# Attention maxima turned on VectorE instead of TensorE, row placing moved to GpSimd

## The chip, the cores and the metric

The kernel runs on one core of one Trainium2 chip. The metric is the device time of one launch in microseconds (us). The kernel before has a median of 676.17 us over 3 runs (671.06 to 678.32). Lower is better.

## The reference

Inputs are 8 sequences ("batches") of 512 tokens with 128 features. What is computed, all in float32:

```python
x = layernorm(x + attn(x))      # 16 heads of 8 features, softmax over 512 keys
# experts: 1 shared, 8 routed, 2 chosen for each token
gates = sigmoid(x @ Wg)
vals, idx = top_k(gates, 2);  vals = vals / vals.sum()
shared = silu(x @ Ws1) * (x @ Ws3) @ Ws2
routed = sum over chosen e of w[e] * (silu(x @ We1[e]) * (x @ We3[e])) @ We2[e]
out = layernorm(x + (shared + routed) / 3)
```

The 16 heads are made from the rows of the projection by a reshape, so a "head" of a batch is 32 tokens' worth of projected rows. The kernel works on them in groups of four: 32 groups in all, four for each batch.

## The kernel before, in words

The program is written engine by engine, with semaphores by hand. Its first part is attention, and a second part after it is the experts. `run_stages` gives every engine the same order: one *stage* (b, i) for each group, i = 0 to 3 within batch b, unrolled at both ends and a loop over batches 2 to 6 between. A stage has eight steps (`at` = 0 to 7).

In stage q = 4b + i TensorE does three things for three different groups. It computes the scores of group q+2 with queries on the partitions (`scoreA`, L1014), only so that VectorE can take their maxima per query (`mx`, L948). It computes the scores of group q with keys on the partitions (`scoreB`, L1028), for which two extra rows of the query stack `qs` hold the negated maximum in a high and a low bf16 part; ScalarE takes the exponential (L921). And in every odd step it multiplies group q-1's exponentials with the values (`pvp`, L1053). Beside these run *jobs* that share one PSUM bank `shared` in a fixed order (class `Jobs`): a job may overwrite the bank only when the job before it has been read. The job `mT` in step 1 turns the 128 x 16 maxima of group q+1 by a TensorE transpose (L532), and VectorE writes their high and low parts from PSUM to `m2` (L607, L609). Other jobs are `xT`, `qkv`, `valsT`, `oT`, `proj`, `x1T` (step 5 of i = 3, needs `x1`), `counts` (step 4 of i = 1) and `gate`.

The path of a group to its scores: the `qkv` job in step 6 of stage q makes queries and keys of group q+4; GpSimd splits them into three bf16 parts (L848 to L854) and adds the bias to the values (L863). In the next stage SyncE (SP) stores the parts to DRAM (L756), loads the maxima into `qs` (`load_maxima`, two transfers, L762), waits until the store has landed, and loads the stacks `qs` and `ks` (eight transfers, L778 and L782). `scoreA` of the stage after that waits for all eight. SP works strictly in this order; in stages i = 0 it also loads `xres` (four transfers) and stores `x1` (four transfers) behind the stacks, and these run into stage i = 1.

GpSimd's order within stage i: for i = 2 first `deviation` (L647, L649); for i = 3 a wait for that stage's stack loads and two indirect scatters of rows (L499, wait and all); then the split, the value bias; for i = 0 `copy_rows` and the `xres` bias; for i = 2 and 3 three more scatters each. The scatters write a batch's rows into expert slots. VectorE computes the slots: `choose` picks two experts for each token (eight pieces, two after every odd step of i = 0), `read_counts` copies the counts in step 4 of i = 1, and `place` turns them into slot numbers and carries the state on (five pieces in i = 1 and 2, L421 to L480). VectorE also normalizes `x1` in i = 3 (L639).

Of the kernel before, what the change touches and what calls it, by code (L numbers as in the profile page):

```python
# [50 lines left out]
class Jobs:  # L51
# [9 lines left out]
    def __init__(self, batches):  # L61
        self.quads = 4 * batches
        self.batches = batches
        self.index = {}
        n = 0
        for s in range(-4, self.quads + 4):
            for at in range(8):
                for kind, b, i in self.at(s // 4, s % 4, at):
                    self.index[kind, 4 * b + i] = n
                    n += 1  # L70
        self.total = n
        self.period = self.index["mT", 12] - self.index["mT", 8]

    def at(self, b, i, at):

        inner = not isinstance(b, int)
        s = 4 * b + i if not inner else 8
        early = not inner and s in (-2, -1)
        kinds = []
        if at == 0 and i == 2 and (inner or 1 <= b <= self.batches):  # L80
            kinds.append("proj")
        if at == 5 and i == 3 and (inner or 1 <= b <= self.batches):
            kinds.append("x1T")
        if at == 1 and (inner or 0 <= s + 1 < self.quads):
# [27 lines left out]
def layer(nc, x, w_qkv, b_qkv, w_out, b_out, wg, ws1, ws3, ws2, we1, we3, we2, out):  # L112
# [27 lines left out]
    with ctx:  # L140
# [47 lines left out]
        mx = sb("mx", [P, 2, 4, NCH])  # L188
        m2 = sb("m2", [16, 2, P], BF16)
        v_raw = sb("v_raw", [P, 4, NCH, HD])  # L190
# [76 lines left out]
        msplit_step = sem("msplit_step")  # L267
        m_loaded = sem("m_loaded")
        v_ready = sem("v_ready")
        b_ready = sem("b_ready")  # L270
# [13 lines left out]
        const_done = sem("const_done")  # L284
        route_step = sem("route_step")
        ids_done = sem("ids_done")
        scattered = sem("scattered")
# [4 lines left out]

        SPLITS = [(QUADS - 2, at) for at in (1, 3, 5, 7)] + [(QUADS - 1, at) for at in (1, 3, 5, 6, 7)]
        ROUTE_STEPS = 44
        CHOSEN = 14
        PLACED = 38

        def need(eng, s, value):
# [21 lines left out]
        def run_stages(eng, stage):  # L320
# [6 lines left out]
            for s in range(QUADS - 4, QUADS + 1):  # L327
                stage(s // 4, s % 4)

        def choose(dve, b, at):  # L330

            def done(n):
                dve.wait_ge(route_step, ROUTE_STEPS * b + n)

# [4 lines left out]
            if at == 0:  # L339

                dve.tensor_scalar(tmp[:], ge[:], 1.0, None, ALU.add).then_inc(route_step, 1)
                done(1)
# [46 lines left out]
        def read_counts(dve, b, bank, read):  # L389

            dve.wait_ge(route_step, ROUTE_STEPS * b + 17)
            dve.tensor_copy(before[:], bank[:, 0:NCH * E].rearrange("p (t e) -> p t e", e=E)) \
               .then_inc(route_step, 1)
            dve.wait_ge(route_step, ROUTE_STEPS * b + 18)
            dve.tensor_copy(count[:], bank[:, NCH * E:2 * NCH * E].rearrange("p (t e) -> p e t", e=E)) \
# [9 lines left out]
        def place(dve, b, at):  # L405
# [5 lines left out]
            def done(n):  # L411
                dve.wait_ge(route_step, ROUTE_STEPS * b + n)

# [56 lines left out]
            else:  # L470
# [10 lines left out]
                done(ROUTE_STEPS)  # L481

        def copy_rows(pool, b):

# [9 lines left out]
        def scatter_rows(pool, b, copies):  # L494

            need(pool, route_step, ROUTE_STEPS * b + PLACED)
            for n in copies:
# [10 lines left out]
        def pe_job(pe, kind, b, i):  # L508
# [6 lines left out]
            elif kind == "qkv":  # L515
# [6 lines left out]
                if has(b, i, 1):  # L522
                    for h in range(4):
                        for low in range(4):
# [3 lines left out]
                                            start=True, stop=True)  # L528
            elif kind == "mT":

                pe.wait_ge(max_done, 8 * (q + 2))
                ins = pe.transpose(shared[0:16, 0:P], mx[:, (i + 1) % 2].rearrange("p h q -> p (h q)"), ident[:])  # L532
            elif kind == "valsT":
# [16 lines left out]
            elif kind == "counts":  # L550
                pe.wait_ge(route_step, ROUTE_STEPS * (b - 2) + CHOSEN)
                ins = count_rows(pe, shared)
# [6 lines left out]
        def act_job(act, kind, b, i):  # L559
# [21 lines left out]
            elif kind == "gate":  # L581

                need(act, route_step, ROUTE_STEPS * (b - 2) + 1)
                act.activation(ge[:].rearrange("p t e -> p (t e)"), shared[:, 0:NCH * E], ACT.Exp,
                               scale=-1.0).then_inc(job_read, 1)

        def dve_job(dve, kind, b, i):
            q = 4 * b + i
            dve.wait_ge(job_ready, jobs.number(kind, b, i) + 1)
            if kind == "valsT":  # L590
# [6 lines left out]
                if i == 2:  # L597
# [5 lines left out]
                    .then_inc(job_read, 1)  # L603
            elif kind == "mT":

                need(dve, m_loaded, 32 * (q + 1))
                dve.tensor_scalar(m2[:, 0, :], shared[0:16, 0:P], -1.0, None, ALU.mult).then_inc(msplit_step, 1)  # L607
                need(dve, msplit_step, q + 2)
                dve.scalar_tensor_tensor(m2[:, 1, :], shared[0:16, 0:P], -1.0, m2[:, 0, :], ALU.mult,  # L609
                                         ALU.subtract).then_inc(job_read, 1)  # L610
            elif kind == "proj":
# [94 lines left out]
        def attention_sync(sp):  # L706
# [36 lines left out]
            def stage(b, i):  # L743
# [61 lines left out]
        def attention_gpsimd(pool):  # L805
# [27 lines left out]
            def stage(b, i):  # L833
                q = 4 * b + i
                if finishing(b) and i == 2:
                    deviation(pool, b)
                if scattering(b) and i == 3:
# [20 lines left out]
                if has(b, i, 1):  # L858
# [5 lines left out]
                                       bv[:, None].broadcast_to([P, 4, NCH, HD]), ALU.add).then_inc(v_ready, 1)  # L864

                if routing(b) and i == 0:
# [34 lines left out]
        def attention_scalar(act):  # L901
# [3 lines left out]
            def stage(b, i):  # L905
# [8 lines left out]
                for j in range(4):  # L914
                    for u in range(2):
# [7 lines left out]
                        for kind, bb, ii in jobs.at(b, i, 2 * j + u):  # L923
                            if kind not in ("valsT", "proj", "mT", "counts"):
                                act_job(act, kind, bb, ii)
# [8 lines left out]
        def attention_vector(dve):  # L934
# [8 lines left out]
            def stage(b, i):  # L943
                q = 4 * b + i
                for at in range(8):
                    if has(b, i, 2):
                        dve.wait_ge(a_ready, 8 * (q + 2) + at + 1)
                        dve.tensor_reduce(mx[:, i % 2, at // 2, at % 2 * 2:at % 2 * 2 + 2], scoreA[:, at % 2], AX.X,  # L948
                                          ALU.max).then_inc(max_done, 1)
                    for kind, bb, ii in jobs.at(b, i, at):  # L950
                        if kind in ("valsT", "proj", "mT"):
                            dve_job(dve, kind, bb, ii)
# [4 lines left out]
                    if i == 0 and at % 2 and routing(b):  # L957
                        if at == 1:
                            dve.wait_ge(job_read, jobs.number("gate", b - 1, 3) + 1)
                            dve.wait_ge(const_done, CONSTS)  # L960
                        choose(dve, b - 2, at - 1)
                        choose(dve, b - 2, at)
                    if i == 1 and at == 4 and routing(b):
                        read_counts_job(dve, b)
                    if i == 1 and at >= 5 and routing(b):
                        place(dve, b - 2, at - 5)
                    if i == 2 and finishing(b):
                        statistics(dve, b, at)
                    if i == 2 and at >= 5 and at % 2 and routing(b):
                        place(dve, b - 2, at // 2 + 1)  # L970
                    if i == 3 and finishing(b):
                        normalize(dve, b, at)
                    if isinstance(b, int) and (q, at) in SPLITS:
# [14 lines left out]
        def attention_tensor(pe):  # L988
# [11 lines left out]
            def stage(b, i):  # L1000
# [18 lines left out]
                def score_b(at, c):  # L1019

                    if has(b, i, 0):
                        j, kc = at // 2, at % 2 * 2 + c
                        if at == 0 and c == 0:

                            pe.wait_ge(m_loaded, 32 * (q + 1))

# [504 lines left out]
        def moe_tensor(pe):  # L1531
# [14 lines left out]
            def beside(n):  # L1546
# [3 lines left out]
                if n == COUNT_AT:  # L1550

                    pe.wait_ge(job_read, jobs.total)
                    pe.wait_ge(route_step, ROUTE_STEPS * (B - 1) + CHOSEN)
                    count_rows(pe, shared).then_inc(counts_ready, 1)
# [147 lines left out]
```

## Time and profile before

| what | value |
|---|---|
| median of 3 runs | 676.17 us (671.06 to 678.32) |
| the profiled execution, its own time | 675.15 us |
| its span, first to last instruction | 673.4 us |
| mean granted TensorE clock | 0.978 |
| PE busy | 631.1 us, 94% |
| VectorE busy | 547.1 us, 81% |
| ScalarE busy | 426.1 us, 63% |
| GpSimd busy | 269.0 us, 40% |

The span is one execution on the chip. "Busy" is the time in which at least one instruction of that engine was under way; matmuls overlap, so a busy PE is not a PE at its peak. PE is the matmul, PEld its weight load, DVE VectorE, ACT ScalarE, POOL GpSimd, SPq the transfers that SyncE issues. Idle time of an engine stands in brackets with what ended it. Attention runs from the start to about 489 us, the experts from there to the end.

### The profile page before, as it was taken

To read this page: it belongs to the slowest core of one execution; us is meant where nothing else is said; L and a number is where in the kernel's file an instruction comes from. 1 tells how busy PE (TensorE), PEld (TensorE's weight loads), DVE (VectorE), ACT (ScalarE), POOL (GpSimd) and SP (SyncE) were. 2 spreads that over 40 slices of the span, in tenths; PEclk is the share of its full clock that TensorE was granted. 3 is DMA by queue.
4 is the path that set the end of the run, shared out by engine and by line. 5 is a ranking of instruction groups with operands and counts; after the bars stand their busy time and mean duration, and the time that the engine had idled before them with its cause. 6 is when DMAs were issued, how large, how long until landed. Compare 5 with 4: busy or idle time off the path is not lost.

```text
span 673.4 us, 16169 instructions
## 1 busy us (share of the span) xinstructions
PE 631.1 (94%) x4643; PEld 321.9 (48%) x4643; DVE 547.1 (81%) x1271; ACT 426.1 (63%) x970; POOL 269.0 (40%) x403
## 2 busy tenths in 40 slices
PE   7899899999999999999999999999899989999990
PEld 4443333433433433343343334423248878888880
DVE  4897677879897997999899799888648757788884
ACT  2066577777676776767776776776744336676672
POOL 3313112232144335414443531450524416677774
PEclk7999899999999999999999999999979999999996
DMA  4557646444433423533333343240231032446433
GB/s 84 124 118 168 139 115 141 105 84 106 74 77 89 93 51 71 104 78 77 75 78 58 84 99 77 63 95 2 59 115 52 29 80 84 119 119 181 133 110 106
DMA packets 161969, 62.61 MB, mean 93 GB/s; under 512 B 110570, under 2 KB 155628, under 8 KB 161920
## 3 DMA queue, kind: packets, MB, share of 16 engines
q1 hardware_dynamic: 155008, 46.66, 32.4%
q0 software_dynamic: 5616, 13.26, 6.6%
q10 hardware_dynamic: 1296, 2.10, 0.9%
q8 instruction: 24, 0.39, 0.3%
q14 instruction: 25, 0.20, 0.1%
HBM read 37.97 MB, written 24.19 MB: 92 GB/s over the span
## 4 chain that ended last, share of the span: by engine, by line
PE 61%; DVE 9%; DMA 9%; issue 8%; POOL 6%; SPq 4%; ACT 3%; POOLq 0%; ACTq 0%; DVEq 0%
PE pvp L1053 16%; PE scoreB L1028 14%; PE scoreA L1014 13%; DVE mx L948 4%; DMA parts_dram<-parts 4%; POOL y_dram L1246 4%; ACT prob L921 2%; PE shared L536 2%; DMA prob<-y_dram 2%; PE scoreB L1643 2%; PE shared L525 1%; PE pvp L997 1%; DMA ks<-parts_dram 1%; PE shared L544 1%; SPq L782 1%
## 5 line engine op out<-in xcount | busy, mean ns | idle before, releaser
L948 DVE TENSOR_REDUCE mx<-scoreA 128x2 f32<-128x1024 f32 x256 | 306.6, 1219 | 60.6 <-PE scoreA L1014 57.6
L921 ACT ACTIVATE prob<-scoreB 128x512 f32<-128x512 f32 x512 | 278.4, 599 | 118.5 <-PE scoreB L1028 118.1
L1014 PE MATMUL scoreA<-ks,qs 72*128 72x512 bf16 x512 | 193.9, 384 | 7.5 <-DMA ks<-parts_dram 4.9
L1028 PE MATMUL scoreB<-qs,ks 74*128 74x512 bf16 x512 | 195.0, 383 | 4.7 <-ACT prob L921 2.1
L1053 PE MATMUL pvp<-prob,v 128*32 128x512 f32 x1024 | 139.2, 617 | 0.8 <-ACT pv_sb L913 0.8
L1014 PEld LDWEIGHTS scoreA<-ks,qs 72*128 72x128 bf16 x512 | 49.4, 99 | 141.0 <-DVE mx L948 55.9
L1028 PEld LDWEIGHTS scoreB<-qs,ks 74*128 74x128 bf16 x512 | 49.3, 98 | 79.5 <-ACT prob L921 54.0
L1246 POOL DMA_INDIRECT y_dram<-prob x71 | 69.8, 983 | 42.0 <-issue 27.3
L499 POOL DMA_INDIRECT slots_dram<-rows,slot_i x64 | 63.2, 988 | 56.4 <-DMA ks<-parts_dram 31.3
L848 POOL CAST parts<-qk 128x256 bf16<-128x256 f32 x32 | 12.7, 397 | 176.2 <-ACT v_raw L574 165.0
L1643 PE MATMUL scoreB<-w,prob 128*128 x284 | 43.4, 276 | 0.3 <-DVE prob L1432 0.3
L1503 ACT ACTIVATE prob<-scoreA 128x256 f32<-128x256 f32 x71 | 27.3, 384 | 24.7 <-PE pvp L1631 12.3
L1053 PEld LDWEIGHTS pvp<-prob,v 128*32 128x32 f32 x1024 | 20.4, 108 | 36.3 <-issue 34.7
L1643 PEld LDWEIGHTS scoreB<-w,prob 128*128 128x128 f32 x284 | 37.2, 191 | 0.5 <-issue 0.5
L1621 PE MATMUL scoreA<-w_high,ebT_high 128*128 x71 | 34.0, 479 | 1.5 <-DVE gated L1436 1.5
L1510 ACT ACTIVATE prob<-scoreB,prob 128x128 f32<-128x128 f32 x71 | 26.1, 368 | 11.4 <-PE scoreA L1601 10.3
L570 ACT ACTIVATE qk<-shared,bq 128x128 f32<-128x128 f32 x64 | 20.0, 364 | 18.3 <-PE shared L525 10.7
L1436 DVE TENSOR_TENSOR gated<-scoreA,prob 128x256 f32<-128x256 f32 x71 | 29.7, 419 | 1.4 <-ACT prob L1503 1.3
L647 POOL TENSOR_SCALAR veps<-mv 128x4 f32<-128x4 f32 x8 | 1.8, 228 | 70.1 <-DVE mv L629 70.1
L1358 DVE TENSOR_TENSOR ebT_low<-scoreA,ebT_high 128x128 fp32r<-128x128 f32 x71 | 20.5, 290 | 11.3 <-ACT ebT_high L1477 9.2
L1623 PE MATMUL scoreA<-w_high,ebT_low 128*128 x71 | 28.0, 394 | 0.0
L1622 PE MATMUL scoreA<-w_low,ebT_high 128*128 x71 | 27.9, 393 | 0.0
(178 smaller groups left out, 918.2 us busy)
## 6 DMA issues: line engine op xcount, KB each, us to landing
qs<-parts_dram SPq DMA_DIRECT2D x96, 96.0 KB
parts_dram<-parts SPq DMA_DIRECT2D x32, 192.0 KB
slots_dram<-blank POOLq DMA_DIRECT2D x9, 520.0 KB
prob<-slots_dram SPq DMA_DIRECT2D x71, 65.0 KB, 1.9
ks<-parts_dram SPq DMA_DIRECT2D x64, 64.0 KB
prob<-y_dram SPq DMA_DIRECT2D x7, 512.0 KB
ks<-parts_dram SPq DMA_DIRECT2D x32, 96.0 KB
xin<-in_L_attn_x SPq DMA_DIRECT2D x32, 64.0 KB, 2.3
```

The lines of the kernel that those rows point to most:

```text
L499: pool.indirect_dma_start(slots_dram, bass.IndirectOffsetOnAxis(ap=slot_i[:, j, t:t + 1], axis=0), rows[:, t, j, :], None).then_inc(scatte ...
L921: act.activation(prob[:, i % 2, j, 2 * u + c, :], scoreB[:, c], ACT.Exp, scale=SCALE).then_inc(exp_done, 1)
L948: dve.tensor_reduce(mx[:, i % 2, at // 2, at % 2 * 2:at % 2 * 2 + 2], scoreA[:, at % 2], AX.X, ALU.max).then_inc(max_done, 1)
L1014: ins = pe.matmul(scoreA[:, at % 2, c], qs[0:KR, st, j, qc * P:(qc + 1) * P], ks[0:KR, st, j, :], start=True, stop=True)
L1028: pe.matmul(scoreB[:, c], ks[0:KM, i, j, kc * P:(kc + 1) * P], qs[0:KM, i, j, :], start=True, stop=True).then_inc(b_ready, 1)
L1053: ins = pe.matmul(pvp[32 * h:32 * h + 32, :], v[:, (i - 1) % 2, h, j, :], prob[:, (i - 1) % 2, h, j, :], start=(j == 0), stop=(j == 3))
L1246: pool.indirect_dma_start(y2_dram, bass.IndirectOffsetOnAxis(ap=eb[:, at, D:D + 1].bitcast(I32), axis=0), yo[:, r, :], None, bounds_check= ...
L1436: dve.tensor_tensor(gated[:, r % 4, :], h_bank(r)[:, F:2 * F], silu[:, r % 2, :], ALU.mult) \
L1621: pe.matmul(h, ebT_highs[:, r % 4], high, start=True, stop=False)
L1622: pe.matmul(h, ebT_highs[:, r % 4], low, start=False, stop=False)
L1623: ins = pe.matmul(h, ebT_lows[:, r % 4], high, start=False, stop=True)
L1643: ins = pe.matmul(y_bank(r), gatedT[:, (r - 4) % 4, c * P:(c + 1) * P], w2_flat[:, bass.ds(e * NFC * D + c * D, D)], start=(c == 0), stop= ...
```

## The change

- The job `mT` goes. `turn_maxima` takes its place at step 0 of the stage: VectorE writes the high and low parts of the 128 x 16 maxima from SBUF to `m2` (now 128 x 32) and turns `m2` in blocks of 32 x 32 into `mT`. `load_maxima` reads `mT` in four transfers of 32 rows of 64 bytes each, not two of 16 rows of 256 bytes.
- `choose` is spread over i = 0 and i = 1.
- For all batches but the last two, `place` goes from VectorE to GpSimd: `place_rows` in stage i = 1 (33 instructions, 27 waits on its own steps), `move_state` behind the scatters of i = 3 (8 instructions). The last two batches keep the VectorE version.
- For batches that end inside the attention part, `x1` is normalized on GpSimd in i = 2, and `deviation` moves there too, both behind the split and the value bias.

```diff
-            kinds.append("mT")
...
+        def turn_maxima(dve, q, parity):
+            maxima = mx[:, parity].rearrange("p h q -> p (h q)")
+            dve.wait_ge(max_done, 8 * (q + 1))
+            need(dve, maxima_turned, q)
+            dve.tensor_scalar(m2[:, 0, :], maxima, -1.0, None, ALU.mult).then_inc(msplit_step, 1)
+            need(dve, msplit_step, 2 * q + 1)
+            dve.scalar_tensor_tensor(m2[:, 1, :], maxima, -1.0, m2[:, 0, :], ALU.mult, ALU.subtract) \
+               .then_inc(msplit_step, 1)
+            need(dve, msplit_step, 2 * q + 2)
+            need(dve, m_loaded, 64 * q)
+            dve.transpose(mT[:], m2[:].rearrange("p m x -> p (m x)")).then_inc(maxima_turned, 1)
...
-                    sp.wait_ge(job_read, jobs.number("mT", b, i) + 1)
-                    for m in range(2):
-                        sp.dma_start(qs[KR + m:KR + m + 1, (i + 1) % 4].rearrange("p h x -> p (h x)"), m2[:, m, :]) \
-                          .then_inc(m_loaded, 16)
+                    sp.wait_ge(maxima_turned, 4 * b + i + 2)
+                    rows = qs[KR:KR + 2, (i + 1) % 4].rearrange("m h (c j t) -> m (h c) j t", c=NCH, j=4)
+                    for low in range(4):
+                        sp.dma_start(rows[:, :, low], mT[32 * low:32 * low + 32, :]).then_inc(m_loaded, 16)
...
-                if finishing(b) and i == 2:
-                    deviation(pool, b)
...
+                if finishing(b) and i == 2:
+                    deviation(pool, b)
+                    need(pool, rstd_done, b)
...
+                    for c in range(NCH):
+                        ins = pool.tensor_scalar(x1[:, c, :], res[:, c, :], mv[:, c, 0:1], rstd[:, c:c + 1],
+                                                 ALU.subtract, ALU.mult)
+                    ins.then_inc(x1_done, 1)
                 if routing(b) and i == 0:
                     copy_rows(pool, b - 2)
+                if scattering(b) and i == 1:
+                    need(pool, const_done, CONSTS)
+                    place_rows(pool, b - 2)
                 if scattering(b) and i >= 2:
                     scatter_rows(pool, b - 2, SCATTERED_AT[i, 1])
+                if scattering(b) and i == 3:
+                    move_state(pool, b - 2)
...
+        CHOSEN_AT = {(0, 1): (0, 1), (0, 3): (2, 3), (0, 5): (4,), (0, 7): (5,), (1, 1): (6,), (1, 3): (7,)}
```

The new `place_rows`, cut: every `op` is one GpSimd `tensor_tensor`, and `done(n)` a wait for its n-th step.

```python
pool.memset(scan, 0.0); pool.memset(cum[:, :, 0:1], 0.0)
pool.tensor_copy(cum[:, :, 1], count[:, :, 0])
done(3); op(cum[:, :, 2], cum[:, :, 1], count[:, :, 1], ALU.add)
done(4); op(cum[:, :, 3], cum[:, :, 2], count[:, :, 2], ALU.add)
done(5); op(held2[:], held[:], cum[:, :, 3], ALU.add)
done(6); op(held2[:], held2[:], count[:, :, 3], ALU.add)
...
done(31); op(slot[:], sel[:, :, :, 0], sel[:, :, :, 1], ALU.add)
done(32); pool.tensor_copy(slot_i[:], slot[:]).then_inc(slots_placed, 1)
```

## Rows read from the trace of the kernel before

**Rows 1.** Windows, i = 0 to 3: length, busy PE PEld DVE ACT POOL, clock, DMA.

```profile
380.89:394.35 13.46, 13.35 (x108) 4.84 (x107) 12.44 (x25) 9.93 (x22) 5.62 (x9) 1.00 0.42 93
394.35:409.25 14.90, 14.60 (x116) 5.75 (x115) 13.70 (x32) 10.51 (x23) 5.85 (x12) 1.00 0.40 84
409.25:423.36 14.11, 14.11 (x115) 5.89 (x114) 13.38 (x30) 9.91 (x22) 3.31 (x7) 1.00 0.33 61
423.36:438.35 14.99, 14.87 (x119) 6.15 (x118) 12.09 (x21) 10.68 (x24) 7.38 (x10) 1.00 0.33 71
```

**Rows 2.** Waits over the span: us in total, times, longest.

```profile
PEld scoreA L1014 <- DVE mx L948: 55.9, 72, 1.5
POOL slots_dram L499 <- DMA ks<-parts_dram: 31.3, 5, 6.5
PE scoreA L1014 <- DMA ks<-parts_dram: 4.9, 5, 2.2
```

**Rows 3.** Timeline, PE around a turned maximum and around none: start, length.

```profile
382.52 0.39 PE L1028 MATMUL scoreB<-qs,ks 74*128 74x512 bf16 x1
...
382.95 1.06 PE L1053 MATMUL pvp<-prob,v 128*32 128x512 f32 x8
383.94 0.10 PEld L1014 LDWEIGHTS scoreA<-ks,qs 72*128 72x128 bf16 x1 [0.84 <-DVE mx L948]
...
394.12 0.10 PEld L1014 LDWEIGHTS scoreA<-ks,qs 72*128 72x128 bf16 x1 [0.84 <-issue]
...
399.52 0.38 PE L1028 MATMUL scoreB<-qs,ks 74*128 74x512 bf16 x1
399.83 0.64 PE L1053 MATMUL pvp<-prob,v 128*32 128x512 f32 x4
```

**Rows 4.** Groups by line in that batch: busy us, mean ns.

```profile
L609 DVE SCALAR_TENSOR_TENSOR m<-shared,m 16x128 bf16<-16x128 f32 x4 | 1.1, 278 | 0.1
```

**Rows 5.** Timeline of SyncE's transfers, stages i = 0 and 1.

```profile
383.25 0.38 SPq L756 DMA_DIRECT2D parts_dram<-parts  x1
384.43 1.93 SPq L762 DMA_DIRECT2D qs<-m  x2
387.23 1.18 SPq L778 DMA_DIRECT2D qs<-parts_dram  x3
...
398.01 0.39 SPq L756 DMA_DIRECT2D parts_dram<-parts  x1
398.51 2.60 SPq L762 DMA_DIRECT2D qs<-m  x2
401.99 1.16 SPq L778 DMA_DIRECT2D qs<-parts_dram  x3
```

**Rows 6.** Timeline, a stage whose end waits for its stack loads.

```profile
173.34 1.16 SPq L778 DMA_DIRECT2D qs<-parts_dram  x3
...
179.13 0.39 PE L1014 MATMUL scoreA<-ks,qs 72*128 72x512 bf16 x1 [0.58 <-DMA ks<-parts_dram]
```

**Rows 7.** Groups by line, small GpSimd instructions: busy us, mean ns.

```profile
L863 POOL TENSOR_TENSOR v<-v_raw,bv 128x128 f32<-128x128 f32 x32 | 14.7, 458 | 21.8 <-ACT valsT L578 11.1 <-issue 10.7
L1233 POOL TENSOR_TENSOR prob<-prob 128x4 f32<-128x4 f32 x7 | 1.5, 210 | 0.6
```

**Rows 8.** Timeline of GpSimd around stages i = 1 to 3.

```profile
410.44 0.46 POOL L863 TENSOR_TENSOR v<-v_raw,bv 128x128 f32<-128x128 f32 x1
420.36 1.05 POOL L649 TENSOR_TENSOR rstd<-veps,half 128x4 f32<-128x4 f32 x1 [0.18 <-POOL veps L647]
422.61 0.40 POOL L848 CAST parts<-qk 128x256 bf16<-128x256 f32 x1 [1.20 <-ACT v_raw L574]
435.59 0.96 POOL L499 DMA_INDIRECT slots_dram<-rows,slot_i  x1 [6.04 <-DMA ks<-parts_dram]
```

**Rows 9.** Timeline of VectorE beside a GpSimd instruction with two inputs.

```profile
406.90 0.21 DVE L444 TENSOR_TENSOR pos<-before,cum 128x32 f32<-128x32 f32 x1
408.44 0.67 DVE L450 TENSOR_TENSOR tmp<-pos,room 128x32 f32<-128x32 f32 x1
```

More of the change, by code:

```diff
@@ L268, in layer @@
         m_loaded = sem("m_loaded")
+        maxima_turned = sem("maxima_turned")
         v_ready = sem("v_ready")
@@ L481, in place, with place_rows, done, per_expert @@
                 done(ROUTE_STEPS)
+        def place_rows(pool, b):
+            def done(n):
+                need(pool, place_step, PLACE_STEPS * b + n)
+            def per_expert(ap):
+                return ap[:, :, None].broadcast_to([P, E, NCH])
+            def by_tile(ap):
+                return ap[:, None, :].broadcast_to([P, NCH, E])
+            def op(out, x, y, what):
+                pool.tensor_tensor(out, x, y, what).then_inc(place_step, 1)
+            scan = g2[:].rearrange("p t e -> p (t e)")[:, 0:2 * (4 + E)].rearrange("p (a x) -> p a x", a=2)
+            first = sel[:, 0].rearrange("p t e -> p (t e)").rearrange("p (e t) -> p e t", t=NCH)
+            need(pool, job_read, jobs.number("counts", b + 2, 1) + 1)
+            pool.memset(scan, 0.0).then_inc(place_step, 1)
+            pool.memset(cum[:, :, 0:1], 0.0).then_inc(place_step, 1)
+            pool.tensor_copy(cum[:, :, 1], count[:, :, 0]).then_inc(place_step, 1)
+            done(3)
+            op(cum[:, :, 2], cum[:, :, 1], count[:, :, 1], ALU.add)
+            done(4)
+            op(cum[:, :, 3], cum[:, :, 2], count[:, :, 2], ALU.add)
+            done(5)
+            op(held2[:], held[:], cum[:, :, 3], ALU.add)
+            done(6)
+            op(held2[:], held2[:], count[:, :, 3], ALU.add)
+            op(first, cum[:], per_expert(held[:]), ALU.add)
+            done(7)
+            op(shift2[:], held2[:], room[:], ALU.subtract)
+            done(9)
+            op(fits[:], per_expert(shift2[:]), limits[:, None, :].broadcast_to([P, E, NCH]), ALU.subtract)
+            op(pos[:], before[:], first.rearrange("p e t -> p t e"), ALU.add)
+            done(10)
+            pool.tensor_scalar(fits[:], fits[:], 0.0, None, ALU.is_gt).then_inc(place_step, 1)
+            done(11)
+            op(tmp[:], pos[:], by_tile(room[:]), ALU.subtract)
+            done(12)
+            op(fits[:, :, 0:2], fits[:, :, 0:2], fits[:, :, 2:4], ALU.add)
+            done(13)
+            pool.tensor_scalar(tmp[:], tmp[:], 0.0, None, ALU.is_ge).then_inc(place_step, 1)
+            done(14)
+            op(more[:], fits[:, :, 0], fits[:, :, 1], ALU.add)
+            op(scan[:, 0, 4:], fits[:, :, 0], fits[:, :, 1], ALU.add)
+            done(15)
+            op(pos[:], pos[:], by_tile(shift[:]), ALU.add)
+            done(17)
+            op(scan[:, 1, 4:], scan[:, 0, 4:], scan[:, 0, 3:3 + E], ALU.add)
+            done(19)
+            op(scan[:, 0, 4:], scan[:, 1, 4:], scan[:, 1, 2:2 + E], ALU.add)
+            done(20)
+            op(ends[:], scan[:, 0, 4:], scan[:, 0, 0:E], ALU.add)
+            done(21)
+            op(ends[:], ends[:], end[:].broadcast_to([P, E]), ALU.add)
+            done(22)
+            op(shift2[:], ends[:], more[:], ALU.subtract)
+            done(23)
+            pool.tensor_scalar(shift2[:], shift2[:], float(P), None, ALU.mult).then_inc(place_step, 1)
+            done(24)
+            op(shift2[:], shift2[:], room[:], ALU.subtract)
+            done(25)
+            op(shift2[:], shift2[:], shift[:], ALU.subtract)
+            done(26)
+            op(tmp[:], tmp[:], by_tile(shift2[:]), ALU.mult)
+            done(27)
+            op(pos[:], pos[:], tmp[:], ALU.add)
+            done(28)
+            op(sel[:], hot[:], pos[:, None].broadcast_to([P, TOP_K, NCH, E]), ALU.mult)
+            done(29)
+            op(sel[:, :, :, 0:4], sel[:, :, :, 0:4], sel[:, :, :, 4:8], ALU.add)
+            done(30)
+            op(sel[:, :, :, 0:2], sel[:, :, :, 0:2], sel[:, :, :, 2:4], ALU.add)
+            done(31)
+            op(slot[:], sel[:, :, :, 0], sel[:, :, :, 1], ALU.add)
+            done(32)
+            pool.tensor_copy(slot_i[:], slot[:]).then_inc(slots_placed, 1)
@@ new lines, in move_state, with done @@
+        def move_state(pool, b):
+            def done(n):
+                need(pool, place_step, PLACE_STEPS * b + n)
+            used, added = fits[:, :, 0], fits[:, :, 2]
+            pool.tensor_scalar(used, more[:], 0.0, None, ALU.is_gt).then_inc(place_step, 1)
+            pool.tensor_scalar(added, more[:], float(P), None, ALU.mult).then_inc(place_step, 1)
+            done(33)
+            pool.tensor_tensor(shift2[:], shift2[:], used, ALU.mult).then_inc(place_step, 1)
+            done(34)
+            pool.tensor_tensor(room[:], room[:], added, ALU.add).then_inc(place_step, 1)
+            done(35)
+            pool.tensor_tensor(shift[:], shift[:], shift2[:], ALU.add).then_inc(place_step, 1)
+            pool.tensor_copy(held[:], held2[:]).then_inc(place_step, 1)
+            pool.tensor_copy(end[:], ends[:, E - 1:E]).then_inc(place_step, 1)
+            pool.tensor_copy(all_ends[:, bass.ds(b, 1), :], ends[:, None, :]).then_inc(place_step, 1)
+            done(PLACE_STEPS)
@@ L945, in stage @@
                 for at in range(8):
+                    if at == 0 and has(b, i, 1):
+                        turn_maxima(dve, q + 1, (i + 1) % 2)
                     if has(b, i, 2):
```

71 lines of the change are left out of this document (40 added, 31 removed).

## The prediction

> **What bounds the kernel now.** I read the busy times first (the table above), then the windows of one batch, then the waits, then the timeline of single stages. PE is busy 94% of the span, VectorE 81%. One batch of the loop takes 57.46 us in four stages, 13.46 + 14.90 + 14.11 + 14.99, and in each PE is busy for all but 0.0 to 0.3 us, while VectorE has 12.09 to 13.70 us to do [rows 1]. So PE is full and VectorE nearly. The waits seem to blame VectorE: `scoreA` waits 55.9 us, 72 times, for the maxima [rows 2]. But the single wait is always 0.84 us, with VectorE named or with nothing named [rows 3]: it is the time that the four `pvp` matmuls in front of it take (382.95 to 383.94), and a late maximum would lengthen it. In the loop VectorE holds nothing up; work taken from it is worth nothing there by itself.
>
> What stands close behind PE is the path of a group's stacks. Where it ends last it holds `scoreA` up, 4.9 us in 5 waits over the span [rows 2], and GpSimd waits for the same loads before its scatters in i = 3, 31.3 us in 5 waits. How near it is in the loop: SP stores the parts at 383.25 and issues the first stack load at 387.23, 3.98 us later [rows 5]. In a stage that did wait, the first load went out at 173.34 and `scoreA` started at 179.13, 5.79 us later [rows 6]. For i = 0 that gives 387.23 + 5.8 = 393.0, and `scoreA` started at 394.12 [rows 3]: 1.1 us to spare. For i = 1, 401.99 + 5.8 = 407.8 against 409.25 - 0.2: 1.3 us.
>
> **Part 1, the turned maxima.** On PE one transpose goes from each stage. From the last `scoreB` to `pvp` it was 0.43 us with it (382.52 to 382.95) and 0.31 without a job (399.52 to 399.83) [rows 3]: 0.12 us a stage, 32 x 0.12 = 3.8 us. In i = 1 the next job no longer waits for VectorE to read the bank; the stage's PE is idle for 14.90 - 14.60 = 0.30 us [rows 1], I allow half, 0.15, six times, 0.9 us. So PE gives back 4.7 us at most.
>
> On VectorE the two reads of PSUM (0.28 each [rows 4]) give way to three dependent small instructions in front of the first maximum. A small one takes 0.21 alone and 0.67 beside a GpSimd instruction with two inputs [rows 9], and GpSimd's split runs just then (422.61 on, against the stage at 423.36 [rows 8, 1]). So 0.6 to 2.0 us, against 0.56 before; VectorE's load falls anyhow (part 3), and I cost it at nothing. If its cover went, `scoreA` of step 2 would be late, by at most 1 us a stage. The Trainium skill ("SBUF — State Buffer", the two separate sides) says that this pair of ports is locked for a whole instruction, and against either engine; the 0.67 agrees for VectorE, and no row shows GpSimd held up.
>
> On SP two transfers become four, between the parts' store and the stack loads. The rows say what they cost: after the store at 398.01 the two ended at 401.11 (398.51 + 2.60), after that at 383.25 they ended at 386.36, both 3.1 us after the store, though issued 0.5 and 1.2 us after it [rows 5]. So SP is held to about 2.5 us behind the store and then takes 0.6 us each. Four end at 3.1 + 2 x 0.62 = 4.34 us, and with 0.2 us for the next wait the loads start 4.55 us behind the store, not 3.98: **0.57 us later in each stage**. Bounds: 0 (if the small transfers cost half as much) and 1.2 us (all of them behind the landing). I take 0.57, the nearest rows.
>
> **Part 2, the stage path with that.** Stages i = 2 and 3 have room and gain PE's 0.12 each. In i = 3 the stack lands 0.57 later and GpSimd's two scatters (435.59 on [rows 8]) with it, and the next stage starts 0.12 earlier: the split of i = 0, which starts when they are done, and the store move from 2.36 us into the stage (383.25 - 380.89) to 3.05. From store to the next stage is 4.55 + 5.8 = 10.35, so i = 0 takes 13.40, PE alone asks for 13.34. In i = 1 the store comes where SP gets to it, 14.76 us behind that of i = 0 (398.01 - 383.25), now 15.33. Both stages together: 3.05 + 15.33 + 10.35 = 28.73 us against 28.36 (13.46 + 14.90). Stages i = 2 and 3: 14.11 + 14.99 - 0.24 = 28.86. The batch: 57.59 against 57.46. **What PE gives, SP takes back: +0.1 us a batch**, for five batches 0.7 us. Ahead of the loop the five waits for stacks [rows 2] would each grow by 0 to 0.57; I take two of them, 1.1 us, less 7 stages at 0.12, 0.8. The last batch, almost without stacks to load, keeps PE's gain: 4 x 0.12 + 0.15 = -0.6. Parts 1 and 2: 0.7 + 1.1 - 0.8 - 0.6 = +0.4, between -4.7 (nothing of SP's shows) and +5 x 1.4 (all 1.2 us show).
>
> **Part 3, placing on GpSimd.** 33 instructions: 19 of 8 elements or about that at 0.21, 11 of 32 or 64 at 0.27 to 0.33 (between 0.210 for 4 and 0.458 for 128 elements [rows 7]), 3 others at 0.2: 7.6 us. Of the 27 waits 19 follow right on the awaited step, and such a gap is 0.18 (420.36 [rows 8]): 3.4 us. Sum 11.0; bounds 8.7 (all at 0.19, fewer gaps) and 14.3 (all at 0.27, 27 gaps of 0.2). It starts behind the value bias at 410.90 and must be over when the split of i = 2 begins, 422.61 [rows 8]: 11.7 us, 11.55 with a stage 0.15 shorter. So it just fits. Each us beyond delays that split, the stack, the scatters, the split of i = 0 and thus the two full stages: one us a batch, five times. I take it 0.3 us over, for its first wait (0.18) and operands in three dimensions, whose price no row shows: +1.4. By the rule on the ports it would be held up besides, by each two-input instruction of VectorE that it meets.
>
> The normalization (4 x 0.35 estimated from 0.458 for 128 elements with two inputs) and `deviation` (1.5) follow the bias and end some 5.6 us into i = 3; `x1T` stands at step 5, over 7 us in. Covered. `move_state` (8 x 0.21 + 4 x 0.18 = 2.4) ends 10 us into i = 0, before the split at 12.6. What VectorE loses (about 6 us of `place` and 1.3 of `x1` a batch) covered nothing. The experts' part keeps its VectorE version and does not move.
>
> **Sum.** 675.15 (the profiled execution, 1.0 below the median) + 0.4 + 1.4 = **677 us**, no change within 1%, which is about what a measurement of this kernel can tell.
>
> **Rivals.**
> 1. *GpSimd's placing does not fit* (slower). From 11.55 us on each us costs 5. At 14.3 it is 2.7 us over: 675.5 + 5 x 2.75 = 689. Its place is the split of i = 2 at 422.61. For it: the length is built of waits, and at about 13.5 us `x1T` loses its cover too. Against: the sum of 11.0. Chance 0.30.
> 2. *SP's extra transfers hide* (faster, a little). They are ready early and cost under 0.3 us each: then PE's 4.7 us stay, 675.15 - 4.7 = 670.5; a little less waiting ahead of the loop brings it to 668. For it: the landing of the store, not the issue, ends most waits. Against: the 0.6 us of rows 5. Chance 0.20.
> 3. *VectorE was the bound after all* (faster by over 1%). If the stages i = 1 and 2, where it is busy 13.70 of 14.90 and 13.38 of 14.11 [rows 1], shrank by 0.8 each: 675 - 6 x 1.6 - 4.7 = 661. Against it the constant 0.84. The Trainium skill ("GPSIMD Engine Reference", when to use it) puts elementwise work on VectorE as the faster one, which speaks against the move, not for it. Chance 0.08.
> 4. Forecast as worked out: 0.42.
>
> **How the numbers follow.** Within 1% (668.4 to 681.9) lie the forecast, most of rival 2 and the mildest of rival 1: 0.42 + 0.13 + 0.02 = 0.57. Faster: rival 3 and the best of rival 2, 0.08 + 0.07 = 0.15. Slower: the rest of rival 1, 0.28. The range 667 to 690 leaves out rival 3 and the worst of rival 1.
>
> **What would show it.** After: `mx` as late as before against `scoreA`; the first stack load 4.5 us behind the store; i = 0 and 1 together 28.4 to 29 us with `scoreA` waiting for the stacks; GpSimd's placing 10.5 to 12 us long, ending near the split. The forecast is wrong if the stack loads still start 4.0 us behind the store, if the placing is over 12.5 us, or if i = 1 gets under 14.5 us.

## The result: 0.6% slower, and the profile after

The changed kernel takes 679.62 us (median of 20 runs, 671.87 to 682.71), the kernel before, timed on the same chip, 675.33 us (20 runs, 670.98 to 682.92). The ratio is 1.0063 with a 95% interval of 1.0042 to 1.0085: slower by about 4 us, within the 1% that counts as no change. The forecast was 677 us and no change.

The profiled execution of the changed kernel took 682.71 us, its span is 681.0 us; it is the longest of the 20 runs, and about 3 us of its span come from a longer stretch at half clock near the start, told of below. So the loop's stages are compared, not the spans. First the windows of one batch after, columns as in [rows 1]:

```profile
387.04:401.22 14.18, 13.32 (x106) 4.74 (x105) 12.50 (x24) 10.51 (x22) 8.62 (x20) 1.00 0.39 82
401.22:416.25 15.03, 14.40 (x114) 5.75 (x114) 12.18 (x21) 10.45 (x22) 5.55 (x11) 1.00 0.41 90
416.25:430.16 13.91, 13.91 (x114) 5.81 (x114) 11.75 (x21) 9.66 (x22) 8.41 (x38) 1.00 0.31 62
430.16:445.04 14.88, 14.77 (x118) 6.13 (x117) 11.35 (x16) 10.68 (x24) 10.61 (x15) 1.00 0.35 67
```

Stages i = 2 and 3 are 0.20 and 0.11 us shorter than before, as PE's missing transposes would have it. Stages i = 0 and 1 are 0.72 and 0.13 longer, although PE works less in them (13.32 and 14.40 against 13.35 and 14.60 [rows 1]): 0.86 us of i = 0 is idle PE, 0.11 before. Over the four, VectorE is busy 3.8 us less (47.78 against 51.61) and GpSimd 11.0 us more (33.18 against 22.16).

The waits over the span (columns as in [rows 2]) name what PE is idle for:

```profile
PE scoreA L1147 <- DMA ks<-parts_dram: 12.9, 14, 2.3
PEld scoreA L1147 <- DVE mx L1084: 40.6, 48, 1.7
```

`scoreA` waits for the stack loads 14 times, 12.9 us, where it was 5 times and 4.9 us [rows 2]. The wait for the maxima, 55.9 us before, is smaller; as then, most of these are the constant 0.84 of `pvp`. In the timeline of PE, at the end of i = 0:

```profile
399.62 0.61 PE L1186 MATMUL pvp<-prob,v 128*32 128x512 f32 x4
400.98 0.39 PE L1147 MATMUL scoreA<-ks,qs 72*128 72x512 bf16 x1 [0.75 <-DMA ks<-parts_dram]
```

SyncE's transfers in the same two stages, to be read against [rows 5], and its stack loads in i = 3:

```profile
390.43 0.39 SPq L876 DMA_DIRECT2D parts_dram<-parts  x1
390.95 4.00 SPq L883 DMA_DIRECT2D qs<-mT  x4
395.30 1.17 SPq L898 DMA_DIRECT2D qs<-parts_dram  x3
...
406.00 0.40 SPq L876 DMA_DIRECT2D parts_dram<-parts  x1
406.51 3.62 SPq L883 DMA_DIRECT2D qs<-mT  x4
410.49 1.17 SPq L898 DMA_DIRECT2D qs<-parts_dram  x3
...
438.20 1.84 SPq L902 DMA_DIRECT2D ks<-parts_dram  x5
```

From the store to the first stack load it is 4.87 and 4.49 us, where it was 3.98 and 3.98 [rows 5]. The four transfers end 4.52 and 4.13 us behind the store, and 0.35 later the first load goes out. Last, GpSimd's new work, first and last lines of placing (33 instructions), then what follows:

```profile
417.48 0.12 POOL L518 MEMSET g<- 128x24 f32 x1
...
424.58 0.20 POOL L513 TENSOR_TENSOR shift<-shift 128x8 f32<-128x8 f32 x1 [0.18 <-POOL shift L513]
424.96 0.25 POOL L513 TENSOR_TENSOR tmp<-tmp,shift 128x32 f32<-128x32 f32 x1 [0.18 <-POOL shift L513]
...
427.51 0.19 POOL L577 CAST slot_i<-slot 128x8 int32<-128x8 f32 x1 [0.17 <-POOL slot L513]
429.41 0.40 POOL L966 CAST parts<-qk 128x256 bf16<-128x256 f32 x1 [1.71 <-ACT v_raw L688]
...
434.66 3.14 POOL L992 TENSOR_SCALAR x<-res,mv,rstd 128x128 f32<-128x128 f32 x4 [0.64 <-POOL rstd L769]
...
443.57 0.96 POOL L617 DMA_INDIRECT slots_dram<-rows,slot_i  x1 [1.92 <-DMA ks<-parts_dram]
...
445.78 0.41 POOL L966 CAST parts<-qk 128x256 bf16<-128x256 f32 x1
```

Placing takes 427.70 - 417.48 = 10.2 us and is over 1.71 us before the split of i = 2 can begin. The split of i = 0 starts at 445.78, 0.74 us into the stage; before, it started 0.53 us ahead of it. (On average over four batches: 0.56 into the stage, and 0.37 ahead of it before.)

### The profile page after: what moved, and what is told of

Read it like the earlier page. It is cut to its first block, busy times and chain, and to the rows that moved or that the text cites. A ratio compares the mean times of both kernels' runs of the same rounds, so it can differ in the third digit from the quotient of the medians.

```text
span 681.0 us, 16556 instructions
## 1 busy us (share of the span) xinstructions
PE 630.9 (93%) x4613; PEld 321.4 (47%) x4613; DVE 527.1 (77%) x1119; ACT 427.6 (63%) x970; POOL 344.1 (51%) x677
## 3 DMA queue, kind: packets, MB, share of 16 engines
q0 software_dynamic: 5616, 13.26, 6.8%
## 4 chain that ended last, share of the span: by engine, by line
PE 44%; SPq 16%; DMA 11%; issue 10%; POOL 8%; DVE 7%; ACT 3%; POOLq 0%; ACTq 0%; DVEq 0%
PE pvp L1186 10%; PE scoreB L1161 9%; PE scoreA L1147 9%; SPq L883 6%; DMA ks<-parts_dram 5%; POOL y_dram L1379 3%; DMA parts_dram<-parts 3%; SPq L902 3%; DVE mx L1084 3%; SPq L898 2%; DMA prob<-y_dram 2%; POOL slots_dram L617 2%; SPq L775 2%; ACT prob L1055 2%; SPq L912 2%
## 5 line engine op out<-in xcount | busy, mean ns | idle before, releaser
L1147 PE MATMUL scoreA<-ks,qs 72*128 72x512 bf16 x512 | 194.8, 386 | 15.6 <-DMA ks<-parts_dram 12.9
L1643 ACT ACTIVATE prob<-scoreB,prob 128x128 f32<-128x128 f32 x71 | 26.1, 368 | 11.4 <-PE scoreA L1734 10.2
L1047 ACT ACTIVATE pv_sb<-pvp 128x512 f32<-128x512 f32 x31 | 18.5, 597 | 12.9 <-PE pvp L1186 12.9
```

The costliest lines, as they stand in the source:

```text
L1147: ins = pe.matmul(scoreA[:, at % 2, c], qs[0:KR, st, j, qc * P:(qc + 1) * P], ks[0:KR, st, j, :], start=True, stop=True)
```

## The experiments

The theories. **S**: SP's four transfers, which stand between the parts' store and the stack loads, take PE's gain and more. **G**: GpSimd's placing and normalization take it. **V**: work taken from VectorE is worth something. Kernels that were timed side by side share the runs of the kernel before; each ratio is to those. "Batch" is the mean of the four loop batches from stage 12 to stage 27, four stages each: 57.48 us before, 58.33 after.

**1. The turned maxima alone**, everything else as before:

```diff
-                pe.wait_ge(max_done, 8 * (q + 2))
-                ins = pe.transpose(shared[0:16, 0:P], mx[...], ident[:])
+                        turn_maxima(dve, q + 1, (i + 1) % 2)
-                    for m in range(2):
-                        sp.dma_start(qs[KR + m:KR + m + 1, ...], m2[:, m, :])
+                    for low in range(4):
+                        sp.dma_start(rows[:, :, low], mT[32 * low:32 * low + 32, :])
```

> The kernel before with the turned maxima and SP's four transfers alone; choice, placing and x1 stay on VectorE as before. Theory S (SP's four transfers make the stacks late in i = 0 and 1): the cost is here. First stack load 4.5 to 4.9 us behind the store, i = 0 and 1 together 28.7 to 29.2 us (before 28.36), i = 2 and 3 0.1 shorter each; ratio to before 1.002 to 1.007. Theory G (GpSimd's longer list of work makes the split late): as before or faster by PE's 0.12 us a stage, ratio 0.994 to 0.999.

Measured: 676.77 us (12 runs) against 672.95, ratio 1.0068 (1.0032 to 1.0103). The whole loss is in this part. The four transfers, the loads and the waits are those of the whole change:

```profile
386.67 0.39 SPq L758 DMA_DIRECT2D parts_dram<-parts  x1
387.19 4.00 SPq L765 DMA_DIRECT2D qs<-mT  x4
391.54 1.17 SPq L780 DMA_DIRECT2D qs<-parts_dram  x3
```

```profile
PE scoreA L1018 <- DMA ks<-parts_dram: 12.2, 14, 1.7
```

Store to load is 4.87 us and the batch 58.30.

**2. The moves alone**: placing, `x1` and the state on GpSimd, the choice over two stages, and the maxima turned on TensorE as before.

```diff
+            kinds.append("mT")
...
-                        turn_maxima(dve, q + 1, (i + 1) % 2)
```

> The change without the turned maxima: the transpose stays on TensorE with two transfers, while the choice is spread, and the placing and x1 go to GpSimd. Theory S: nothing of it is on the path, ratio 0.998 to 1.002, stages as before to 0.1 us, first stack load 3.98 us behind the store. Theory G: the slowdown is here, ratio 1.004 to 1.008, with the split of i = 2 or of i = 0 later than before. Theory V (VectorE was a bound): faster, i = 1 and 2 shorter by 0.5 us or more, ratio under 0.99.

Measured: 672.98 us against 672.95, ratio 0.9987 (0.9962 to 1.0012). G falls, and V with it for the stages of the loop. The window of its stage i = 1, columns as in [rows 1]:

```profile
395.23:410.05 14.82, 14.44 (x115) 5.83 (x114) 11.69 (x20) 10.55 (x23) 5.83 (x12) 1.00 0.43 89
```

VectorE has 2.0 us less to do in i = 1 (11.69 against 13.70 [rows 1]) and the stage is 0.08 us shorter. One stage outside the loop does gain from the moves: stage 29, in the last batch, takes 13.26 us instead of 14.29.

**3. The whole change with the four transfers issued by ScalarE**, one in each of steps 1 to 4, behind the exponentials of the step:

```diff
-                if has(b, i, 1) and not ramp:
-                    load_maxima()
+                        if has(b, i, 1) and 2 * j + u in (1, 2, 3, 4):
+                            if 2 * j + u == 1:
+                                act.wait_ge(maxima_turned, q + 2)
+                            low = 2 * j + u - 1
+                            act.dma_start(rows[:, :, low], mT[32 * low:32 * low + 32, :])
```

> The changed kernel with its four transfers of the maxima issued by ScalarE's queue, one behind each of steps 1 to 4, not by SP. Theory S: the first stack load is again 4.0 us behind the store, the waits for stacks in i = 0 and 1 go, a batch takes 56.7 to 57.0 us, ratio to before 0.990 to 0.996. Theory G: as the changed kernel, 1.004 to 1.008. A cost of its own is possible: each issue holds ScalarE up by some tenths of a us, and scoreB waits for its exponentials.

Measured: 670.31 us against 672.95, ratio 0.9959 (0.9922 to 0.9996), with a batch of 56.84 us and the loads on average 4.0 to 4.2 us behind the store. With SP's four transfers gone the loss turns into a gain: S again.

**4. Two transfers ahead of the store, two behind**, both still on SP. Behind a store SP issues nothing for about 2.5 us anyway, so two transfers there should be free.

```diff
+                if has(b, i, 1) and not ramp:
+                    load_maxima(range(2))
                 if has(b, i, 3):
...
-                    load_maxima()
+                    load_maxima(range(2, 4))
```

> The changed kernel with two of SP's four transfers ahead of the parts' store and two behind it. Theory S: behind the store it is as before, first stack load 4.0 us after it; but the two ahead take 1.3 us of SP where SP is late already (i = 1), so the store of i = 1 comes as much later as its stack load comes earlier. i = 0 shorter by 0.5 to 0.9 against the changed kernel, i = 1 as there; ratio to before 0.998 to 1.004, below the changed kernel's 1.006. Theory G: 1.004 to 1.008.

Measured: 685.71 us (6 runs), ratio 1.0191 (1.0143 to 1.0239): a miss. The loads do start 3.97 us behind the store, but the store of i = 1 is late itself:

```profile
395.23 0.39 SPq L886 DMA_DIRECT2D parts_dram<-parts  x1
399.20 1.18 SPq L900 DMA_DIRECT2D qs<-parts_dram  x3
...
409.29 0.38 SPq L834 DMA_DIRECT2D xin<-in_L_attn_x  x1
409.77 1.41 SPq L875 DMA_DIRECT2D qs<-mT  x2
411.45 0.40 SPq L886 DMA_DIRECT2D parts_dram<-parts  x1
```

The two ahead (409.77 to 411.18) stand in front of a store whose parts GpSimd had finished at 407.06: the distance between the two stores is 16.22 us, 14.76 before and 15.57 after. i = 1 takes 16.14 us. That SP comes late to the store of i = 1 was in the expectation; it had i = 0 shorter and i = 1 as in the changed kernel. On average i = 0 takes 13.38 us (14.20 after) and i = 1 16.33 (15.36): together 29.71 against 29.56. The store of i = 1 comes a set distance behind that of i = 0 (16.22 to 16.28 us in four batches), whenever the stage begins, so what i = 0 gains i = 1 loses, and nothing is left. Stage i = 2 is 0.8 us longer on average: it takes 15.5 us in the two of four batches where a stretch of 3.4 us at half clock lies in it, 13.9 in the others. Two more such stretches lie ahead of stage 12 (65.5 and 123.5), where the kernel before, from stage 0 on, has one (80.4). In i = 1, issues ahead of the store cost in full; those behind it are free up to its landing: with two of them the loads start 3.98 us behind it, as in the kernel before.

**5. Each of the four transfers in two halves**, eight issues:

```diff
                     for low in range(4):
-                        sp.dma_start(rows[:, :, low], mT[32 * low:32 * low + 32, :])
+                        for m in range(2):
+                            part = mT[32 * low + 16 * m:32 * low + 16 * m + 16, :]
+                            sp.dma_start(rows[m:m + 1, :, low], part)
```

> The changed kernel with each of SP's four transfers of the maxima cut in two (16 rows of 64 bytes each): same bytes, eight issues. Theory S: SP pays about 0.65 us for each issue beyond the first, so the first stack load is 7.2 to 7.6 us behind the store (changed kernel 4.6 to 4.9); all of i = 0, 1 and 3 wait for stacks, a batch takes 63 to 68 us, 700 to 720 us in all. If bytes or rows were what costs, not issues: as the changed kernel, 679.

Measured: 744.91 us (2 runs), ratio 1.1059 (1.1008 to 1.1109).

```profile
436.08 0.38 SPq L876 DMA_DIRECT2D parts_dram<-parts  x1
436.57 6.40 SPq L885 DMA_DIRECT2D qs<-mT  x8
443.32 1.16 SPq L900 DMA_DIRECT2D qs<-parts_dram  x3
```

Store to load 7.24 us, 2.37 more than with four: 0.6 us for each issue more. The batch has 66.66 us. The step was as expected; the total lies higher. The granted clock of the run is 0.927, against 0.977 in the change: in time at half clock that is an estimated 54 us lost ((1 - 0.927) x 743) instead of 16, and the 38 us between them bring the 745 to 707 (more on the clock below).

**6. The turned maxima alone, from ScalarE's queue**: experiment 1 with the transfers of experiment 3, nothing moved to GpSimd.

> The kernel before with the turned maxima alone, their four transfers issued by ScalarE's queue. Theory S: what TensorE gives (0.12 us a stage and some tenths in i = 1) is kept, ratio 0.993 to 0.998, as the variant with the moves to GpSimd; the moves are worth nothing. Theory V (work taken from VectorE counts once SP is out of the way): slower than that variant by 0.3% or more.

Measured: 671.27 us against 673.90, ratio 0.9946 (0.9921 to 0.9971), not to be told from experiment 3. But its batch is 57.32 us and that of experiment 3 56.84, so the pair was timed again (9 and 10).

**7. The kernel before, with its two transfers issued by ScalarE** in steps 2 and 3, TensorE turning the maxima:

```diff
-                        sp.dma_start(qs[KR + m:KR + m + 1, (i + 1) % 4]..., m2[:, m, :])
+                            act.dma_start(qs[KR + m:KR + m + 1, (i + 1) % 4]..., m2[:, m, :])
```

> The kernel before, its TensorE transpose kept, with its two transfers of the maxima issued by ScalarE's queue. If SP's queue was on the path before the change too: ratio 0.994 to 0.998, and the turned maxima are worth little by themselves. Theory S as the prediction has it (1.1 us to spare in i = 0 and 1 before): 0.999 to 1.001 in the loop; only the stages that waited for stacks gain.

Measured: 676.18 us against 673.90, ratio 1.0005 (0.9966 to 1.0043). Loads on average 3.97 to 4.04 us behind the store, as before. So two transfers were hidden by the store, and another queue alone brings nothing; what experiments 3 and 6 gain is PE's.

**8. Placing made longer** by eight dependent additions on GpSimd (128 x 8 each, their result is not used):

```diff
+            for k in range(EXTRA):
+                op(cum[:, :, 3], count[:, :, 3], count[:, :, 3], ALU.add)
+                done(k + 1 - EXTRA)
             pool.memset(scan, 0.0).then_inc(place_step, 1)
```

> The changed kernel with eight more dependent GpSimd instructions at the head of the placing (8 x 0.39 = 3.1 us, their results are not used): 10.2 becomes 13.3 us, 1.6 to 1.8 us more than fits ahead of the split of i = 2. By the prediction's term of one us a batch for each us too much, five times: +8 to +9 us on the changed kernel, a batch 60 us, 687 in all. If the wait for the stack in i = 3 (1.9 us in the changed kernel) takes it up: under +2 us.

Measured: 688.06 us (4 runs), ratio 1.0245 (1.0195 to 1.0295), 1.8% over the change; batch 60.77 us.

```profile
433.16 0.19 POOL L581 CAST slot_i<-slot 128x8 int32<-128x8 f32 x1 [0.17 <-POOL slot L514]
433.61 0.40 POOL L970 CAST parts<-qk 128x256 bf16<-128x256 f32 x1 [0.26 <-issue]
...
438.88 3.16 POOL L996 TENSOR_SCALAR x<-res,mv,rstd 128x128 f32<-128x128 f32 x4 [0.64 <-POOL rstd L773]
```

```profile
442.18 0.63 PE L667 MATMUL shared<-ident,x 128*128 128x128 f32 x4 [1.46 <-POOL x L996]
```

```profile
PE shared L667 <- POOL x L996: 5.4, 6, 1.5
```

The split of i = 2 now starts right behind the placing, 1.28 us into i = 3 instead of 0.75 ahead of it. So everything behind it on GpSimd is 2.03 us later. The split itself hardly shows (i = 0 takes 14.40 us on average, 14.20 after); what shows is `x1T`, which lost its cover. After, it had 0.6 us to spare (`x1` ready at 437.80, turned from 438.39); 2.03 - 0.59 = 1.44, and the wait is 1.46. Stage i = 3 takes 15.94 us on average against 14.86. With i = 0 that is 1.3 us a batch. Of the rest of the batch's 2.4 us, 0.9 is one stage i = 1, with a stretch of 10.2 us at half clock from 400.1 on: it takes 19.33 us, the other three 15.57 on average, and the 3.8 between them are spread over four batches. The other 0.2 is in these three (15.57 against 15.36 after).

**9 to 11. Experiment 3, experiment 6 and the change itself, side by side**, to price the moves once SP is out of the way.

> The whole change with the four transfers of the turned maxima issued from ScalarE's queue (the kernel of the third experiment), now timed side by side with the same without the moves to GpSimd. Theory M (the moves are worth something once SP is out of the way): in the profile of the version without them, PE waits 0.49 us longer for a maximum in each stage i = 1, because VectorE's choice pieces at the end of i = 0 and its turn stand in front of the first maximum. With the moves there is no such wait: i = 1 takes 14.72 against 15.20, five loop batches and a few ends, 2.4 to 3 us. So this one at 0.992 to 0.996 of before and 0.3 to 0.5% faster than its partner. Rival N (GpSimd's placing and normalization give it back elsewhere): both alike within 0.1%.

> Turned maxima from ScalarE's queue, placing, normalization and choice as before (the kernel of the sixth experiment). Theory M: 0.3 to 0.5% slower than its partner, 0.996 to 0.999 of before, batch 57.3 us, with the wait of 0.49 us in each i = 1. Rival N: within 0.1% of its partner.

> The changed kernel itself beside these two: 1.005 to 1.008 of before again, and 1.0 to 1.4% over the version with ScalarE's transfers, if SP's four transfers are its whole loss. A profile without a long stretch at half clock near the start should show the span at 674 to 678.

Measured, 12 runs each against 672.98 us: with the moves 668.05, ratio 0.9938 (0.9913 to 0.9962); without them 672.03, 0.9989 (0.9958 to 1.0020); the change 678.13, 1.0067 (1.0038 to 1.0095). The moves are worth 0.5% here, V after all. Experiments 3 and 6, the same two kernels timed apart, did not show it (0.9959 and 0.9946, each known to some 0.3%), so the size rests on this pair and on the traces. The window of i = 1 with the moves, then without:

```profile
388.30:403.01 14.71, 14.32 (x114) 5.74 (x113) 12.65 (x23) 10.55 (x23) 5.93 (x12) 1.00 0.41 90
```

```profile
389.20:404.40 15.20, 14.40 (x114) 5.81 (x113) 14.12 (x33) 10.50 (x23) 5.87 (x12) 1.00 0.42 86
```

Only i = 1 differs, by 0.49 us; i = 0 takes 13.35 us in both. Its start without the moves, on VectorE and then on PE:

```profile
389.01 0.18 DVE L375 TENSOR_TENSOR hot<-iota_e,pick 128x32 f32<-128x32 f32 x1
...
390.40 0.17 DVE L612 TENSOR_SCALAR m<-mx 128x16 bf16<-128x16 f32 x1
390.61 0.57 DVE L614 SCALAR_TENSOR_TENSOR m<-mx,m 128x16 bf16<-128x16 f32 x1
391.31 0.21 DVE L618 STREAM_TRANSPOSE mT<-m 128x32 bf16<-128x32 bf16 x1
391.45 3.46 DVE L946 TENSOR_REDUCE mx<-scoreA 128x2 f32<-128x1024 f32 x3
```

```profile
392.71 0.39 PE L1012 MATMUL scoreA<-ks,qs 72*128 72x512 bf16 x1 [0.50 <-DVE mx L946]
```

The choice runs into i = 1, then comes the turn, and the first maximum starts 2.25 us into the stage; PE then waits 0.50 us for it. With the moves the choice is spread over two stages, the first maximum starts at 389.40, 1.10 us in, and PE does not wait. From stage 12 on this happens five times (4 x 0.49, and 0.49 in the last batch), 2.5 us, and stage 11 takes 15.80 instead of 14.85: 3.4 of the 4.0 us between the medians. Experiment 9 is also the version that beats both kernels: 0.6% under the one before, and 1.3% under the change by the two ratios (0.9938 / 1.0067).

## Why the forecast was right, step by step

The sum was near (677 against 679.6), and the mechanism that was named likeliest is the one that the runs show: SP takes back more than PE gives. That the sum came so near is in part luck: the batches were put 3.7 us too low and the placing 1.4 us too high.

- **PE is the bound, VectorE holds nothing up.** Right for the loop of the kernel before (experiment 2: no stage there shrinks by more than 0.1 us). It has its limit: with the turn on VectorE and no moves it holds i = 1 up by 0.49 us. The turn was costed at nothing because the moves free VectorE; the price without that cover is within the "at most 1 us a stage" of the forecast.
- **PE's gain**, 4 x 0.12 + 0.15 = 0.63 us a batch. Experiment 9 against before: 57.46 - 56.83 = 0.63 (0.11, 0.19, 0.19 and 0.14 by stage). On average 0.07 of it comes with the moves alone (experiment 2).
- **SP, 4.55 us from store to load instead of 3.98.** Measured 4.87 in i = 0 and 4.49 in i = 1 of the batch above (4.88 and 4.61 on average). The term was mis-sized twice: the four take up to 4.52 us, not 4.34, and the wait behind them 0.35, not 0.2. Rival 2 (they hide) is refuted.
- **The store of i = 0 at 3.05 us.** It came at 3.39, and over four batches at 3.58 (3.37 to 3.92). This is the step that was off most, and for the most part by its start: the 2.36 us of the batch in [rows 5] are the earliest of the four before, which are 2.93, 2.59, 2.89 and 2.36, on average 2.69. So the store moved by 0.89, where 0.69 was forecast. In i = 3 the last stack load is issued 9.88 us into the stage (438.20 + 1.84 - 430.16), before it was 9.16 in, 0.72 later and not 0.57. The scatters start 13.41 us in (443.57 - 430.16), before 12.23 (435.59 - 423.36 [rows 8, 1]); over four batches 13.20 and 12.39, 0.81 later. The loads of that stage before:

```profile
430.69 1.83 SPq L782 DMA_DIRECT2D ks<-parts_dram  x5
```

  From the last issue to the scatter it is 3.53 us here and 3.07 in the batch before, but over four batches it is 3.17 to 3.53 and 3.03 to 3.58, on average 3.33 and 3.23: the landing takes hardly longer, it only varies.
- **Store to next stage 5.8 us behind the load.** 401.22 - 395.30 = 5.92 and 416.25 - 410.49 = 5.76. Right.
- **i = 0 and 1 together 28.73 us, the batch 57.59.** 29.21 in the batch shown, 29.56 on average; the batch 58.33. The 0.83 by its parts: 0.53 from the store of i = 0, 0.24 from the distance between the stores (15.57, not 15.33), the rest from the last load. Five batches make 3.7 us more than forecast.
- **Ahead of the loop +0.3, last batch -0.6.** Up to stage 12 the change, run again, took 207.09 us and the kernel before 208.44; the profiled run of after took 211.72, with 3.4 us lost to its longer stretch at half clock. So this is within what the clock does. The last batch: 50.38 against 50.61, -0.2; what was gained there (48.95 in experiment 9, and 1.03 of its 1.66 is stage 29, where experiment 2 has it too) a first stage of 14.25 us took back.
- **Placing 11.0 us, 0.3 us too long, +1.4.** 10.2 us, 1.7 us to spare, so 0. The gaps of 0.18 were right; instructions on 32 elements take 0.25 and those on 8 take 0.20, where I had 0.27 to 0.33 for the former. Its 3-dimensional operands cost nothing extra. Rival 1 (it doesn't fit) is refuted. In the loop no instruction of the placing is longer than its like (0.20 to 0.24 us for 8 elements), but there VectorE runs beside it only what reads PSUM or has one input. In the last placing that GpSimd does, it meets a VectorE instruction with two inputs in SBUF, and its 8 elements take 0.66 us, the same instruction 0.20 in the loop (at 423.37):

```profile
479.28 0.69 DVE L1074 TENSOR_TENSOR w_low<-w,w_high 128x512 fp32r<-128x512 f32 x1
479.38 0.66 POOL L513 TENSOR_TENSOR shift<-ends,more 128x8 f32<-128x8 f32 x1
```

  It started 0.10 us behind VectorE's and ended 0.07 behind its end. VectorE in its turn takes 0.57 us (390.61 above), beside a GpSimd instruction with two inputs that began at 390.48 and took 0.67, for what takes 0.18 in experiment 9, started while GpSimd pauses (388.96). The rule of the Trainium skill ("SBUF — State Buffer", the two separate sides), that the pair of ports is locked against either engine, agrees with both.
- **Each us beyond the window costs one a batch, by the split of i = 2.** Neither the size nor the place holds (experiment 8): 2.03 us late cost 1.3 a batch, 0.6 for each us, and 1.1 of them are PE's wait for `x1`. The cover of `x1T` ends at a placing of 10.2 + 1.7 + 0.6 = 12.5 us, not 13.5.
- **`x1` ends 5.6 us into i = 3.** It ended 7.64 in (437.80): one of the four takes 0.785 us (3.14 / 4), not the 0.35 that I had estimated. `x1T` began at 438.39, so 0.6 us were left of its cover, where I saw 1.4 and more.
- **Rival 3** (VectorE was the bound, 661): refuted, no stage of the loop in experiment 2 shrank by more than 0.1 us, and stage 29's 1.0 is all that was near it.

Mended, the forecast is 677 + 3.7 for the batches - 1.4 for the placing = 679.3. Both corrections are measured, and the sum leaves out what the clock takes, so its nearness to 679.6 shows only that no large term is missing.

## What to carry to other kernels

Before one transfer becomes several, ask what its queue's engine issues behind it: here each issue costs 0.6 us, those that fit into the 2.5 us behind a large store are free, and those beyond it, or ahead of it where the queue is late already, push a path on which PE waits. Put small transfers on a queue whose engine has slack. And a piece of work that takes load off an engine can be worth nothing until the next limit is gone: measure it with that limit removed, too.

## What the runs showed of the hardware

**Waits of PE and its clock.** After PE has waited for a stack the granted clock is often 0.50, 1.2 instead of 2.4 GHz, for some us. In the changed kernel:

```profile
78.53 0.39 PE L1147 MATMUL scoreA<-ks,qs 72*128 72x512 bf16 x1 [2.27 <-DMA ks<-parts_dram]
...
79.83 0.61 PE L1161 MATMUL scoreB<-qs,ks 74*128 74x512 bf16 x1
```

```profile
79.70:89.90 10.20, 10.17 (x34) 2.83 (x34) 5.14 (x6) 4.14 (x8) 0.00 (x0) 0.50 0.71 130
```

That stage took 17.96 us, 15.01 before, where a wait of 2.15 us was followed by 3.4 us at half clock. In the change run again a wait of 2.41 us stands in such a stretch within the loop:

```profile
222.69 0.60 PE L1147 MATMUL scoreA<-ks,qs 72*128 72x512 bf16 x1 [2.41 <-DMA ks<-parts_dram]
```

```profile
222.00:228.80 6.80, 6.11 (x18) 1.52 (x19) 2.74 (x4) 2.39 (x4) 3.54 (x7) 0.50 0.34 87
```

Its batches average 59.65 us, with 10.2 us at half clock among them, against 58.33 without any. Experiments 7 and 9 have no such stretch within attention and waits of at most 1.6 us; experiment 5, with waits of up to 5.5 us, has twelve. Not every wait brings one: 1.87 us at 62.9 in the changed kernel did not. Nor is a long one needed: the stretch of experiment 8 came 1.2 us after a wait of 1.43. So a wait may at times cost more than its length, which was in no term of the forecast. That this makes the spread between runs is likely, but no run here isolates it.

**ScalarE's queue.** An issue takes 0.62 us there too, but the next exponential starts beside it:

```profile
378.99 0.62 ACTq L1053 DMA_DIRECT2D qs<-mT  x1
379.04 0.59 ACT L1043 ACTIVATE prob<-scoreB 128x512 f32<-128x512 f32 x1
```

**GpSimd with two operands per partition.** `tensor_scalar` with `mv` and `rstd` on 128 x 128 takes 785 ns, one with two full inputs of the same size 458 ns [rows 7].
